# A decoder layer's last stage: routing steps and logits moved beside other tiles, and the routed up weights split into hi and lo parts

## What is computed

```python
scores = softmax(xf @ gate_w.T)                 # 8 experts
weights, idx = top_k(scores, 2)
h = einsum('td,eid->eti', xf, w1)               # for the experts that are picked
g = silu(h) * einsum('td,eid->eti', xf, w3)
eo = einsum('eti,edi->etd', g, w2)
y = weighted sum of eo over a token's two picks
z = silu(xf @ ws1.T) * (xf @ ws3.T) @ ws2.T     # the shared expert, for every token
out = x + y + z
```

## Time and profile before

| | |
|---|---|
| time, median of 3 runs | 1463.16 us (1463.11 to 1467.15) |
| the profiled execution: its time | 1463.24 us |
| the profiled execution: its span from first to last instruction | 1461.2 us |
| what lies around the span | 2.0 us |
| TensorE busy, share of the span | 96% |
| mean granted TensorE clock | 0.988 of 2.4 GHz |
| shared steps 1 to 15 | 1104.6 to 1208.0 us |
| routed products, first to last tile | 1208.0 to 1441.1 us |

### The profile page before, as it was taken

The page is one execution under the profiler, slowest core; times in us unless marked ns, Lnnn a source line. Parts: engine busy times, 40 slices in busy tenths (PEclk is TensorE's granted clock), DMA queues, the critical chain, the costliest instruction groups (busy, mean ns, idle before and its releaser), DMA issues.

```text
span 1461.2 us, 23234 instructions
## 1 busy us (share of the span) xinstructions
PE 1401.7 (96%) x8216; PEld 1069.0 (73%) x8216; DVE 669.5 (46%) x1916; ACT 553.2 (38%) x1104; POOL 498.4 (34%) x485
## 2 busy tenths in 40 slices
PE   8999999999999999999999999999889979999995
PEld 6888888888888888888877877777668865444442
DVE  5788864333332333334566666665665561000000
ACT  4444441111111111111267777777772303333331
POOL 4554450202021120204275454554251023444442
PEclk9999999999999999999999999999999989999998
DMA  6000021101010100101000000000107413555543
GB/s 245 2 0 0 0 87 44 44 1 44 0 44 1 43 10 33 44 0 47 10 18 20 20 20 20 2 20 5 45 30 320 169 44 94 89 88 90 89 88 41
DMA packets 20528, 73.38 MB, mean 50 GB/s; under 512 B 2320, under 2 KB 3344, under 8 KB 18000
## 3 DMA queue, kind: packets, MB, share of 16 engines
q0 software_dynamic: 10176, 25.17, 8.8%
q1 hardware_dynamic: 10256, 46.93, 8.7%
HBM read 52.95 MB, written 19.14 MB: 49 GB/s over the span
## 4 chain that ended last, share of the span: by engine, by line
PE 86%; DVE 7%; ACT 3%; issue 2%; DMA 1%; POOL 1%; DVEq 0%; POOLq 0%; ACTq 0%
PE ps L738 18%; PE ps L740 18%; PE ps L739 18%; PE ps L1134 10%; PE ps L986 5%; PE ps L1171 4%; PE ps L978 2%; PE ps L1010 2%; DVE den L1595 2%; PE ps L1095 2%; ACT cols L1402 1%; PE ps L1115 1%; ACT cols L1390 1%; PE ps L1144 1%; PE ps L1004 1%
## 5 line engine op out<-in xcount | busy, mean ns | idle before, releaser
L738 PE MATMUL ps<-feat,wsplit 128*128 128x512 f32 (+1 forms) x672 | 247.1, 368 | 3.1 <-PE ps L740 2.1
L740 PE MATMUL ps<-feat,wsplit 128*128 128x512 f32 (+1 forms) x672 | 244.5, 364 | 0.0
L739 PE MATMUL ps<-feat,wsplit 128*128 128x512 f32 (+1 forms) x672 | 244.5, 364 | 0.0
L1254 ACT ACTIVATE sg<-ps 128x512 f32<-128x512 f32 x64 | 38.3, 598 | 369.4 <-PE ps L740 369.4
L1780 DVE CUSTOM_DVE_ANT_0 cols<-ps,msk 128x256 f32<-128x256 f32 (+1 forms) x512 | 148.9, 353 | 54.0 <-PE ps L978 33.7
L507 POOL CAST wsplit<-wraw 128x3072 fp32r<-128x3072 f32 x9 | 24.8, 2754 | 399.3 <-PEq L926 386.9
L1515 DVE TENSOR_TENSOR m_f<-ps,sg 128x512 f32<-128x512 f32 x64 | 44.2, 691 | 245.6 <-ACT sg L1254 245.6
L738 PEld LDWEIGHTS ps<-feat,wsplit 128*128 128x128 f32 x672 | 126.7, 189 | 26.4 <-issue 6.6
L1134 PE MATMUL ps<-rawx,hT_x 128*128 x312 | 143.7, 603 | 1.4 <-issue 1.0
L1390 ACT COPY cols<-ps 128x512 f32<-128x512 f32 x192 | 112.3, 585 | 76.9 <-PE ps L986 76.8
L740 PEld LDWEIGHTS ps<-feat,wsplit 128*128 128x128 f32 x672 | 126.7, 189 | 19.9
(11 more groups left out here) (266 smaller groups left out, 2767.8 us busy)
## 6 DMA issues: line engine op xcount, KB each, us to landing
wraw<-weights SPq DMA_DIRECT2D x11, 1536.0 KB, 6.4
rawx<-weights SPq DMA_DIRECT2D x8, 1536.0 KB, 13.5
ctx_raw<-ctx_t SPq DMA_DIRECT2D x8, 512.0 KB, 4.5
h_rows<-hd POOLq DMA_DIRECT2D x16, 256.0 KB, 3.8
out<-acc SPq DMA_DIRECT2D x4, 1024.0 KB, 4.4
qkv_raw<-weights SPq DMA_DIRECT2D x6, 512.0 KB, 7.1
acc<-x SPq DMA_DIRECT2D x1, 3072.0 KB, 17.9
acc<-x SPq DMA_DIRECT2D x2, 512.0 KB, 6.9
```

The costliest lines, as they stand in the source:

```text
L738: nc.tensor.matmul(out_, w_hi, m_hi, start=first, stop=False)
L739: nc.tensor.matmul(out_, w_lo, m_hi, start=False, stop=False)
L740: return nc.tensor.matmul(out_, w_hi, m_lo, start=False, stop=last)
```

## The change

Four things change, all in the last stage. Line numbers below are those of each kernel.

1. The routed up and gate product becomes three fp32r matmuls (`up_x` calls `three`). For that, every routed tile's up weights are split anew: ScalarE copies each half of them as hi (`ux_hi`), VectorE subtracts to get lo (`ux_lo`), into `up_even` or `up_odd` by turns. Both engines read the expert's number into a register of their own first. The transposed input is split too (`hx_lo`). The down product stays as it was.
2. Heads, norms and logits come from three tables; all logits are done by step 5, two heads a step.
3. The routing's steps stand at other places of the loop; `running_counts` moves from step 10 to 7, `slots` from 13 to 12.
4. An add into the output waits for the one before only where the two tiles are of different experts, or past the last used tile (`other_of`, read into a register by GpSimd).

```diff
+HEADS_AT = {0: (6,), 1: (7, 8), 2: (9, 10), 3: (11, 12), 4: (13, 14), 5: (15,)}
+NORMS_AT = {1: (9, 10), 2: (11, 12), 3: (13, 14), 4: (15,)}
+LOGITS_AT = {1: (0, 1, 2, 6), 2: (3, 4, 5, 7, 8), 3: (9, 10, 11, 12), 4: (13, 14), 5: (15,)}
...
-        hT_x = at("hT_x", [P, 2, KB, P], F32, off=split_at + 8 * SLOT)
+        hT_x = at("hT_x", [P, 2, 2, KB, P], F32R, off=split_at + 8 * SLOT)
+
+
+        up_even = at("up_even", [P, 2, UPN], F32R, off=split_at + 8 * SLOT + 2 * 4096)
+        up_odd = wsplit[:, 0, :, 0:UPN]
...
             sp.wait_ge(d["up"], AHEAD)
-            for e in range(2):
-                load_expert(e)
-            for q in range(1, GROUPS):
-                store_x(q)
+            load_expert(1)
+            store_x(1)
+            store_x(2)
+            sp.wait_ge(d["up"], TILES - 2)
+            load_expert(0)
+            store_x(3)
...
-                after(pool, d["added"], 16 * s)
+                after(pool, added[s % 2], 16 * (s // 2))
+                before_ = (s + 1) // 2
+                if 0 < s < 3:
+                    pool.wait_ge(added[(s + 1) % 2], 16 * before_)
+                elif s >= 3:
+
+                    other = pool.value_load(other_of[0:1, s:s + 1], min_val=0, max_val=16)
+                    hold(pool, added[(s + 1) % 2], other + 16 * (before_ - 1), pool_held)
...
+            def up_of(s):
+                return up_odd if s % 2 else up_even
+
+            def up_x(g):
+                s = g - TILES
+                pe.wait_ge(d["hT_x"], s + 1)
                 pe.wait_ge(d["m"], g - 1)
+                w = up_of(s)
                 for k in range(KB):
-                    mm = nc.tensor.matmul(ps[:, g % 2, :], hT_x[:, g % 2, k, :], raw[:, k * 512:(k + 1) * 512], start=(k == 0), stop=(k == KB - 1))
+                    if k % 2 == 0:
+                        pe.wait_ge(d["ux"], 2 * s + k // 2 + 1)
+                    o = slice(k * 512, (k + 1) * 512)
+                    mm = three(pe, ps[:, g % 2, :], hT_x[:, g % 2, 0, k, :], hT_x[:, g % 2, 1, k, :], w[:, 0, o], w[:, 1, o], k == 0, k == KB - 1)
                 mm.then_inc(d["up"], 1)
...
-                if i + AHEAD < TILES:
-                    head_t(i + AHEAD)
+                for g in HEADS_AT.get(i, ()):
+                    head_t(g)
+                if i == 7:
+                    running_counts()
                 if i > TILES - 2 and i + 2 < ALL:
                     head_t(i + 2)
...
                 elif i + 1 < ALL:
+                    up_x(i + 1)
                     raw[i + 1] = raw_of(i + 1)
-                    up_x(i + 1, raw[i + 1])
-                for t in LOGITS.get(i, (i + AHEAD,) if i + AHEAD < TILES else ()):
+                for t in LOGITS_AT.get(i, ()):
                     logits(t)
-                if i == 10:
-                    running_counts()
-                if i == 13:
+                if i == 12:
                     slots()
...
+            def ux_hi(g, half):
+                s = g - TILES
+                if half == 0:
+                    if s == 0:
+                        act.wait_ge(d["experts"], 1)
+                        for e in range(EXPERTS):
+                            act.wait_ge(raw_expert[e], 16)
+                    if s > 0:
+                        act.wait_ge(d["up"], g - 1)
+                    raw[g] = act.value_load(expert_of[0:1, s:s + 1], min_val=0, max_val=EXPERTS - 1)
+                o = slice(half * UPN // 2, (half + 1) * UPN // 2)
+                w = up_odd if s % 2 else up_even
+                nc.scalar.copy(w[:, 0, o], rawx[:, bass.ds(raw[g], 1), o].rearrange("p o n -> p (o n)")).then_inc(d["ux_hi"], 1)
...
-                if i + AHEAD < TILES:
-                    hT_hi_d(i + AHEAD)
+                if i == 3:
+                    exps_d(0)
+                if i == 6:
+                    exps_d(1)
+                for g in HEADS_AT.get(i, ()):
+                    hT_hi_d(g)
                 if i > TILES - 2 and i + 2 < ALL:
                     hT_hi_d(i + 2)
+                    ux_hi(i + 2, 0)
                 if i > TILES:
                     scale_rows(i - 1)
                 if i + 2 == TILES:
                     act.wait_ge(d["inv"], 1)
+                    ux_hi(i + 2, 0)
+                    ux_hi(i + 2, 1)
                 if i + 1 < ALL:
                     silu_d(i + 1)
-                if i == 3:
-                    exps_d(0)
-                if i == 9:
-                    exps_d(1)
                 if i == TILES - 2:
                     hT_hi_d(i + 2)
+                if i > TILES - 2 and i + 2 < ALL:
+                    ux_hi(i + 2, 1)
...
+            def ux_lo(g, half):
+                s = g - TILES
+                dve.wait_ge(d["ux_hi"], 2 * s + half + 1)
+                if half == 0:
+                    raw[g] = dve.value_load(expert_of[0:1, s:s + 1], min_val=0, max_val=EXPERTS - 1)
+                o = slice(half * UPN // 2, (half + 1) * UPN // 2)
+                w = up_odd if s % 2 else up_even
+                nc.vector.tensor_tensor(w[:, 1, o], rawx[:, bass.ds(raw[g], 1), o].rearrange("p o n -> p (o n)"), w[:, 0, o], ALU.subtract).then_inc(d["ux"], 1)
+
+            def hx_lo(g):
+                dve.wait_ge(d["hx_hi"], g - TILES + 1)
+                nc.vector.tensor_tensor(hT_x[:, g % 2, 1, :, :], ps[:, 2 + g % 2, :].rearrange("p (k n) -> p k n", k=KB), hT_x[:, g % 2, 0, :, :],
+                                        ALU.subtract).then_inc(d["hT_x"], 1)
...
+                    stats_group(3)
                     continue
-                if i + AHEAD < TILES:
-                    hT_lo_d(i + AHEAD)
-                if i + 8 < TILES:
-                    h_d(i + 8)
-                if i == 2:
-                    stats_group(3)
-                if i == 4:
+                for g in HEADS_AT.get(i, ()):
+                    hT_lo_d(g)
+                for g in NORMS_AT.get(i, ()):
+                    h_d(g)
+                if i == 5:
                     router_picks(0)
-                if i == 10:
+                if i == 6:
+                    router_probs(1)
                     router_picks(1)
-                if i == 11:
+                if i == 7:
                     slot_bases()
-                if i == 12:
+                if i == 8:
+                    slots_of_picks()
+                if i == 9:
                     tiles_of_picks()
                     lanes_of_picks(0)
+                if i == 10:
                     lanes_of_picks(1)
-                if i == 13:
+                    lanes_of_picks(2)
+                if i == 11:
+                    tokens_of_picks()
                     lanes_of_picks(3)
-                    tokens_of_picks()
+                if i == 12:
+                    experts_of_tiles()
+                if i == TILES - 2:
+                    ux_lo(i + 2, 0)
+                    ux_lo(i + 2, 1)
+                if i > TILES - 2 and i + 2 < ALL:
+                    hx_lo(i + 2)
+                    ux_lo(i + 2, 0)
                 if i + 1 < ALL:
                     mult_d(i + 1)
-                if i == 3:
+                if i == 2:
                     router_max(0)
-                if i == 9:
+                if i == 4:
+                    router_probs(0)
+                if i == 5:
                     router_max(1)
-                if i == 11:
-                    slots_of_picks()
+                if i == 6:
+                    gates_of_picks()
                 if i == 12:
-                    lanes_of_picks(2)
-                if i == 13:
                     slot_table()
                 if i < TILES:
                     dve.wait_ge(d["down"], i + 1)
                     nc.vector.tensor_tensor(acc[:, i, :], ps[:, 4 + i % 2, :], acc[:, i, :], ALU.add).then_inc(d["acc"], 1)
+                if i == TILES - 2:
+                    hx_lo(i + 2)
+                if i > TILES - 2 and i + 2 < ALL:
+                    ux_lo(i + 2, 1)
 
 
 
```

More of the change, by code:

```diff
@@ L265, in decoder_layer @@
         expert_of = at("expert_of", [P, COLS], I32)
+        other_of = at("other_of", [P, COLS], I32)
+        past = at("past", [P, COLS], F32)
         ids_f = at("ids_f", [P, 2, COLS], F32)
@@ L378, in decoder_layer @@
             mT_ps="m transposed in PSUM", mT_hi="its hi", mT="its lo too", down="sums in PSUM", acc="shared sums added to the residual",
-            y="routed sums scaled", hT_x="routed tiles of h transposed in SBUF", mT_x="routed tiles' m transposed in SBUF", added="routed tiles added, by 16",
+            y="routed sums scaled", hx_hi="routed tiles of h transposed, their hi", hT_x="their lo too", ux_hi="halves of a tile's up weights with hi", ux="split", others="whether a tile follows one of another expert", mT_x="routed tiles' m transposed in SBUF",
             pool="GpSimd's own small steps", dve="the vector engine's")
@@ L383, in decoder_layer @@
         raw_expert = [sem(f"d_raw_expert{k}") for k in range(EXPERTS)]
```

(29 more changed lines are left out.)

21 lines of the change are left out of this document (11 added, 10 removed).

## The result

1443.95 us median (1443.64 to 1445.26, 4 runs) against 1463.13 before: ratio 0.9862, interval 0.9848 to 0.9876. The kernel became 1.4% faster, 19 us, where 8 were forecast.

The account below looks back on a forecast made before the run. The prediction took TensorE to bound the kernel (86% of the chain), with waits and clock also costing in the shared steps. 1463.2 - 5.5 (routed) - 3.1 (shared) + 0.4 (ends) = 1455.0 us; whole range 1434 to 1467, forecast's own 1448 to 1462.

Parts of the forecast that it names:

- V: Routed steps: one read of the expert's number plus its register operations, on ScalarE and again on VectorE; 1.12 us each.
- the loop: Routed steps, one m_t to the next through ScalarE and VectorE: 3.61 + 2 V, 5.85 us, setting the step.
- There they cost nothing: Reads on TensorE's queue, 0.673 us in the median, were said to run while older matmuls do.
- Nothing else counts there: Routed steps of the kernel before: TensorE busy 226.5 of 227.8 us at the full clock, so only its work counts.
- rival 1: Routed steps: reads quick, V below 0.81, TensorE sets the step at 5.23 us; 1431.4 us in all; chance 0.20.
- The rest of the routed step has room: Routed steps: ScalarE's new 2 x 1.05 us and VectorE's 2 x 1.22 fit; second halves ready a step ahead.
- The adds ... gain nothing: Routed steps: adds let loose within one expert bring no gain, since TensorE never waited for them.
- Shared steps: Stretch before the routed steps: waits 8.1 us where 8.8 were, plus 2.4 from the clock; 3.1 us gained.
- The clock: Shared steps: four to five low-clock stretches of 1.7 us lose 7.6 us, against 10 in the kernel before.
- The loop longer than before: Routed steps: two reads with V = 1.35 make the step 6.31 us and the time 1472.5; chance 0.17.
- GpSimd locking VectorE out: Routed steps: issuing an indirect DMA excludes VectorE's subtraction, half a microsecond a step, 19 us lost, 1474; chance 0.05.
- The ends: Ends of the routed part: last product 0.7 us shorter, last adds 1.1 us later; net 0.4 us lost.

Follow-up runs that it names:

- e5: The kernel before, with TensorE reading a routed tile's expert number one tile ahead, behind the issue of a product; 1457.85 us, ratio 0.9962.
- e1: The changed kernel with each gather one tile earlier in GpSimd's queue, so an add and a gather change places; 1429.38 us, ratio 0.9763.
- e4: The changed kernel with the routed up product again one fp32 matmul per k, without splitting; shared part and loosened adds kept; 1452.87 us, ratio 0.9921.
- e6: e1 with every add waiting for the one before it, as in the kernel before; 1468.16 us, ratio 1.0023.
- e9: The changed kernel with its adds in series again, gathers left where the change has them; 1468.21 us, ratio 1.0030.
- e3: e1 with VectorE reading the expert's number three times in a row instead of once; 1474.26 us, ratio 1.0081.
- e10: e1 with ScalarE's and VectorE's reads one tile ahead and the adds in series again; 1464.08 us, ratio 0.9999.

## Why the prediction was right or wrong

The direction was right, the time lies in the range, but the gain was 19 us and not 8; it fell outside the forecast's own 1448 to 1462. That it lies in the range at all is partly luck: with the cost of a read put right, the prediction's own sum gives 1431.4 us, below the range's 1434, and a wait that it did not have took it back to 1444.

- **The term that was mis-sized: V.** "With the median V = 1.12, and the loop is 5.85 us" is the step that failed. The reads on ScalarE and VectorE with their register operations took 0.63 and 0.73, the loop 4.97. I took a median of 0.673 from a queue in which nearly every read fell into the stretch behind an add. It was a price of that place, not of a read. The shortest row (0.303), which I kept as a bound, was the right one. The floor of about 600 ns that the Trainium skill, "DMA: Bandwidth & Descriptors", section "Latency and other measured facts", gives does not hold here: the medians are 0.28 to 0.31 on four queues.
- **"There they cost nothing" was wrong** of the kernel before: the slow reads cost it 0.185 us a step, 7 us in all, as e5 shows. "Nothing else counts there" was read from the busy time, which covered these waits. Two of the products in the earlier trace rows have idle time in front of them that "issue" ended, which was the sign.
- **The wait that I missed: the gather.** With V as measured, rival 1's condition (V below 0.81) held, and its step of 5.23 and time of 1431.4 should have come. They came in e1 (5.16 and 1429.4), not in the change, because the loop through ScalarE's scaled rows and GpSimd's add and gather takes 5.57 us in the step shown, 5.54 on average. "The rest of the routed step has room" counted the busy time of ScalarE and VectorE and did not follow GpSimd's queue. This took back 14.6 of 29 us.
- **"The adds ... gain nothing" was wrong here.** It held for the step of before: e5, adds in series, and e4, adds loosened, both have 5.8 us steps. It fails as soon as TensorE's step is shorter than the adds' own chain: 5.80 us in e5, and 6.0 to 6.2 with the split's subtractions on VectorE. In the changed kernel they are worth 1468.2 - 1444.0 = 24 us, more than the whole gain. The argument "TensorE never waited for them" was one of the old step.
- **Shared steps: right, within what these runs can tell.** 3.8 gained for 3.1 forecast. TensorE's waits of steps 1 to 15 were forecast as 8.1 us (1.4, 2.1, 0.4, 2.0, 2.2); the trace has 7.9, and step 6 shows 2.0, step 10 1.9, step 1 1.2 and steps 14 and 15 2.1:

```profile
PE ps L1176 <- DVE m_x L2046: 6.1, 5, 2.0
PE ps L1119 <- DVE hd L1877: 1.2, 1, 1.2
PE ps L762 <- DVE hT_x L2040: 0.6, 1, 0.6
```

- **The clock**: forecast 7.6 us lost; 0.05 x 10.5 + 0.22 x 29.0 = 6.9 by

```profile
1105.46:1116.00 10.54, 9.34 (x62) 8.13 (x60) 6.43 (x15) 2.32 (x5) 2.35 (x4) 0.95 0.95 361
1116.00:1145.00 29.00, 28.50 (x154) 25.21 (x152) 12.11 (x25) 7.92 (x14) 3.25 (x6) 0.78 0.72 298
1145.00:1205.09 60.09, 53.84 (x280) 44.12 (x278) 43.97 (x149) 14.68 (x30) 12.28 (x7) 1.00 0.33 114
```

  The low stretches begin in or right behind the three larger groups of logits, and none is left from step 5 on. With one schedule the shared steps took 96.3 to 100.8 us in these profiles, so 3.8 is uncertain by some 2 us. What each of the moved steps brings was not tried apart.
- **The rivals.** The loop longer than before (0.17): not in the change, but e6 and e9 show its row, reads of 0.82 and 0.88. GpSimd locking VectorE out: no, it is the other way round. The subtraction takes 1.21 to 1.29 us in the changed kernel, also while an add is being issued, and nearly every issue that starts while it runs ends 1.43 to 1.51 us behind its end.
- **The ends**: 0.4 lost was forecast, 1.2 came. The last two tiles are padding, whose adds stay in series as before; which of the prediction's two terms was off was not tried apart.

## What to carry to other kernels

When work is taken off the engine that sets the step, list every loop that returns to it, those through DMA queues too, and price each by itself: here the loops were 4.97 (VectorE), 5.57 (GpSimd's gather behind its add), 6.0 to 6.2 (adds in series) and 5.13 (TensorE), and the longest one left decides. A wait that costs nothing at the old step may be the bound at the new one, so "nobody waits for it now" is no price. New work can also lengthen a loop that it is no part of, as the subtractions on VectorE lengthened GpSimd's adds. And a duration that varies threefold between rows of one line is to be explained by what stands beside the row before its median is used elsewhere.

## What the runs showed of the hardware

- A register read from SBUF takes 0.27 to 0.31 us, in the median, on four engines' queues alike, and its register operations and gaps 0.32 more (VectorE's in e3). In the twelve profiles 151 reads started 0.6 to 1.3 us behind the end of an accumulating indirect DMA's issue: all took longer, 0.40 to 1.01, and 124 of them ended 1.69 to 1.72 behind it. The 150 that started within 0.3 behind the end took 0.27 to 0.32, and the 110 from 1.4 to 1.7 behind it 0.27 to 0.36. Of the 49 in between, from 0.3 to 0.6 behind it, 37 took more than 0.4. What holds them no run shows. A read at the first routed tiles took 0.88 to 0.92 in several runs with no add near it; that stays open too.
- Adds in series stand 6.03 to 6.20 us apart on average in e6, e9 and e10. The order between experts must stay: the Trainium skill, "DMA: Bandwidth & Descriptors", section "Rules for kernel authors", says that an accumulating DMA reads its destination and writes it later with nothing holding the bytes in between. No run here tried it.
- The issue of an add on GpSimd took 1.59 us in the kernel before and up to 2.65 in others (median 1.99 in e6): all 166 that took more than 1.65 started while a 128x1024 subtraction with both inputs in SBUF was running on VectorE, and ended 1.43 to 1.51 us behind the subtraction's end. The gathers show the same: 32 took more than 1.18 us to issue (up to 2.11), all started during such a subtraction and ended 0.88 to 0.96 behind its end; the others took 1.01 to 1.17. The other way round little happened: the 180 subtractions that started during an add's issue took 1.21 to 1.25 us.
